# An attention and feed-forward layer on one core: weight pieces, first rows and last tiles placed elsewhere, the projection spread over four units, its reciprocal root on VectorE

## The chip, the cores and the metric
One core of one Trainium2 chip. The metric is the time of one execution in device microseconds (us); of the kernel before three runs were taken.

## The reference
```
x = h                                              # [8, 1024, 512] f32
qvk = layernorm(x) @ Wqvk                          # 16 heads of 32; order q, v, k
w   = softmax(causal(q k^T) / sqrt(512))
x   = x + layernorm((w v) @ Wo)
t   = layernorm(x) @ W1 + b1                       # 2048 wide
t   = t + (cos(th) wr + sin(th) wi) * wi * sin(th + 0.1 t) * 0.1
x   = x + layernorm(relu(t) @ W2 + b2)             # layernorm: eps 1e-5, no gain or bias
```
th, wr and wi are the quantum phases and weights.

## The kernel before
All products are done in float16 pairs: a number is split in a high and a low half, and three of the four cross products are added (PASSES), so one float32 product is three matmuls. There are three phases, one block each (`qkv_phase`, `attention_phase`, `ffn_phase`), and every engine's order of work is written out by hand; all DMAs are issued by SP, in order, and an engine or SP that waits holds up all that stands behind it.

**QKV** works in 16 chunks of 512 rows. A chunk has 12 products m of 12 matmuls each: 8 for q and k (`stage`, a ring of four, stored to `qk_parts` in DRAM), 4 for v. ScalarE writes the high half, VectorE the low half. Beside them the next chunk's rows are normed, split (`upper`, `lower`) and turned by DMA (`turn`). The chunks from 6 on (PEELED = 5 batches of two chunks, outside the loop) also prepare the weights of the other phases. Nine pieces (Wo, four of W1, four of W2; 1 MB each) pass through three slots: first each is read for its largest magnitude (VectorE, `largest`, and for Wo `centre`), at MAX_CHUNK = 6 and m in MAX_M; then, after `scales` in chunk 9, each is loaded once more and split in halves (`piece_high`, `piece_low`), from chunk 10 at m in SPLIT_M, and stored to DRAM in `weights.parts`. `first_units` loads q, k, v and rows of the first two attention units, all at the head of chunk 9. The last chunk also computes the row maxima of the first unit.

**Attention** works batch by batch; a batch has four units of four heads, a unit 20 slots (STEPS: query columns c of 256, key tiles j). In a slot TensorE makes scores (L1095), ScalarE the exponentials (L1158) and the high half (L1168), GpSimd the low half (L1257, SBUF to SBUF), and TensorE, six slots later, the weighted sum with v (L1122). For the next unit, score pieces are made in `pw` (two banks) and reduced by VectorE (L229): three in each of the first four slots of a unit, one to three in the others up to slot 15. `normalise` and `turned` put the result in `oT`. The output projection of a batch comes as eight tiles of 128 rows, each 12 matmuls in one bank `pwo` (L1080), then on VectorE mean and variance (`wo_stats`), on GpSimd `wo_small` (add eps, power -0.5), on VectorE `wo_out`, and a store to `x1`. The slots are WO_AT = 10, 15, ..., 45, counted from the head of the batch's last unit, so tiles fall into that unit and the first two of the next batch. `Stage` holds the order of the first, the middle, the last batch and of the drain after it; the middle batches 1 to 6 are one loop of six turns. In the drain all tiles follow one another in `pwo`.

**The feed-forward phase** has 16 chunks of 512 rows and 16 column groups f each: `hidden` (L1592), the activation over ScalarE and VectorE, and two groups later `output` (L1602). It starts with its own loads in SP's order: rows of chunk 0, quarters of w1 and w2, turns, the rest of the weights, b2, rows of chunk 1. VectorE scales b2 before its first group. At the end `post_read`, `post_stats` and `post_residual` run over all four tiles of the last chunk, with one store of 1 MB.

Of the kernel before, what the change touches and what calls it, by code (L numbers as in the profile page):

```python
# [29 lines left out]
P = 128  # L30
# [45 lines left out]
MAX_M, SPLIT_M = (1, 5, 9), (3, 9)  # L76
MAX_CHUNK, SCALE_CHUNK, SPLIT_CHUNK = 6, 9, 10
VEC_CHUNK = 6
# [63 lines left out]
assert all(TURN_AT[t // TQ] < at < NS + TURN_AT[t // TQ] for t, at in enumerate(WO_AT))  # L142
TAIL = WO_AT_LAST[-1] + WO_STORE + 1 - NS
# [6 lines left out]
MS = 2.0 ** 14  # L150

# [92 lines left out]
def qkv_phase(nc, x, w_qvk, w_o, w1, w2, vectors, weights, units, qk_parts, v_parts):  # L244
# [6 lines left out]
    LOAD_CHUNK = 9  # L251
    SLOTS = 3
    PEELED = 5
# [16 lines left out]
    with ctx:  # L270
# [72 lines left out]
        def job_at(n, m):  # L343

            for first, chunk, at in ((0, MAX_CHUNK, MAX_M), (PIECES_W, SPLIT_CHUNK, SPLIT_M)):
                if n >= chunk and m in at:
                    piece = len(at) * (n - chunk) + at.index(m)
                    if piece < PIECES_W:
                        return first + piece
            return None  # L350
# [6 lines left out]
        with nc.Block() as block:  # L357
            @block.sync
            def _(sp):
# [87 lines left out]
                def first_units():  # L447
                    for s in stored:
                        sp.wait_ge(s, 16 * (QK // STAGE) * CPB + START)
                    for u in range(2):  # L450
                        for c in range(CPB):
                            load_qk(sp, units, qk_parts, 0, u, c, True)
                            load_qk(sp, units, qk_parts, 0, u, c, False)
                    sp.wait_ge(v_stored, 16 * CPB + START)
                    for u in range(2):
                        load_v(sp, units, v_parts, 0, u)
                    for t in range(2):
                        load_x(sp, units, x.rearrange("b (t p) d -> b t p d", p=P), 0, t)
# [19 lines left out]
                for i in range(BATCH - PEELED, BATCH):  # L478
                    for e in range(2):
# [3 lines left out]
                        if 2 * i + e == LOAD_CHUNK:  # L483
                            first_units()
# [310 lines left out]
            def _(pe):  # L795
# [66 lines left out]
                with pe.Fori(1, BATCH - PEELED) as i:  # L862
                    for e in range(2):
                        chunk(i, e, False)
# [5 lines left out]
class Stage:  # L870
# [16 lines left out]
    def tiles(self, u, k, lag):  # L887

        s = u * NS + k - lag
        for m, (this, before) in enumerate(zip(*self.wo_at)):  # L890
            if s == this + (UNITS - 1) * NS and self.this:
                yield 0, m
            if s == before - NS and self.before:
                yield -1, m

# [43 lines left out]
def attention_phase(nc, x, weights, units, qk_parts, v_parts, x1):  # L939
    PR, HR, YR = 10, 10, 4  # L940


    LIFT = 8 * math.log(2)
    CONST = 2

    ctx = ExitStack()
    with ctx:
# [18 lines left out]
        oT = sb("oT", [P, 2, GROUPS, SEQ], F16)  # L966
# [3 lines left out]
        small = sb("small", [P, YR, 2])  # L970
        half = sb("half", [P, 1])
        y = sb("y", [P, YR, D])
# [12 lines left out]
        stats_done, mv_done, small_done = sem("stats_done"), sem("mv_done"), sem("small_done")  # L985
        wo_done, y_done = sem("wo_done"), sem("y_done")
        y_stored = [sem(f"y_stored{b}") for b in range(YR)]

        x_v = x.rearrange("b (t p) d -> b t p d", p=P)

        with nc.Block() as block:
# [11 lines left out]

            def run_all(engine, run):

                run(0, FIRST)
                with engine.Fori(1, BATCH - 1) as i:
                    run(i, MIDDLE)
                run(BATCH - 1, LAST)
                run(BATCH, DRAIN)  # L1010

            @block.sync
            def _(sp):
                x1_v = x1.rearrange("b (t p) d -> b t p d", p=P)

                def run(i, stage):
                    for u, k in stage.slots:
# [15 lines left out]
                        for b, t in stage.tiles(u, k, WO_STORE):  # L1033
# [4 lines left out]
                            elif stage is not DRAIN:  # L1038
                                load_x(sp, units, x_v, i + b + 1, t + 2 - QT)
                        if k == MAX_AT:  # L1040
# [637 lines left out]
```

## Time and profile before
| | |
|---|---|
| runs | 3446.77 us median of 3 (3444.99 to 3449.8) |
| profiled execution | 3445.31 us, span 3443.5 us |
| TensorE busy | 3148.3 us (91%) |
| VectorE, ScalarE, GpSimd busy | 2237.1 (65%), 2070.4 (60%), 1327.9 us (39%) |
| mean granted TensorE clock | 0.973 |

The busy shares are means over three phases with different limits. In the rows below PE is TensorE, PEld its weight loads, DVE VectorE, ACT ScalarE, POOL GpSimd, SPq the DMA queue's issues; L1095 is line 1095; "idle <- X" says what an engine stood waiting for. Tile names begin with q_, a_, f_ for the three phases, u_ and w_ for what they share.

### The profile page before, as it was taken

The numbers are of one execution on the slowest core, as the hardware profiler recorded it, in microseconds if no ns is written. First come the engines' busy times: TensorE is split into PE (matmuls) and PEld (weight loads), VectorE is DVE, ScalarE is ACT, GpSimd is POOL, SyncE is SP. The second block draws the span as 40 slices with busy tenths as digits, with TensorE's granted clock in tenths as the row PEclk, the third lists the DMA queues.
The fourth block names the chain that finished last, engine by engine and source line by source line (L and its number), as shares of the span: only waits on it lengthen the run. The fifth ranks groups of instructions, "written<-read, shape, count | busy, mean of one in ns | idle before, by whom it ended". The sixth has DMA issues, their size and how long they took to land. (4 is left out here: it accounts for less than half of the span.)

```text
span 3443.5 us, 76542 instructions
## 1 busy us (share of the span) xinstructions
PE 3148.3 (91%) x29476; PEld 1797.2 (52%) x29476; DVE 2237.1 (65%) x4207; ACT 2070.4 (60%) x2451; POOL 1327.9 (39%) x718
## 2 busy tenths in 40 slices
PE   7999898999898989989899858999999999999998
PEld 3444344766666666767676623444444444444443
DVE  5455555777676777767677624666666666666665
ACT  3222332988888887979797924555555555555554
POOL 2000000988888897979798930000000000000000
PEclk9999999999999999999999978999999999999999
DMA  6578783122222222222222132111111111111110
GB/s 181 171 218 248 232 260 90 52 70 82 58 84 64 81 69 78 63 84 58 86 66 79 44 101 90 37 38 39 37 37 37 37 37 37 37 37 37 37 37 25
DMA packets 328304, 279.95 MB, mean 81 GB/s; under 512 B 151056, under 2 KB 270032, under 8 KB 325968
## 3 DMA queue, kind: packets, MB, share of 16 engines
q1 hardware_dynamic: 328016, 275.82, 27.8%
q8 instruction: 217, 3.56, 0.4%
q14 instruction: 71, 0.58, 0.1%
HBM read 148.87 MB, written 92.80 MB: 70 GB/s over the span
## 5 line engine op out<-in xcount | busy, mean ns | idle before, releaser
L1257 POOL TENSOR_TENSOR a_prob_lo<-a_prob,a_prob_hi 128x2048 f16<-128x2048 f32 (+2 forms) x448 | 1191.9, 2689 | 185.8 <-ACT a_prob_hi L1168 184.2
L229 DVE TENSOR_REDUCE u_mx<-a_pw 128x4 f32<-128x512 f32 (+1 forms) x1178 | 730.6, 657 | 166.4 <-PE a_pw L215 126.6
L1158 ACT ACTIVATE a_prob<-a_pst,a_lift,w_exp_scale 128x1024 f32<-128x1024 f32 (+1 forms) x640 | 709.6, 1124 | 207.5 <-PE a_pst L1095 101.4
L1592 PE MATMUL f_ph<-f_xT,f_w 128*128 128x512 f16 x3072 | 707.5, 380 | 26.9 <-DMA f_xT<-f_xh 26.9
L1602 PE MATMUL f_py<-f_w,f_act 128*128 128x512 f16 x3072 | 707.6, 380 | 25.0 <-DVE f_work L1445 12.3
L1168 ACT ACTIVATE a_prob_hi<-a_prob 128x2048 f16<-128x2048 f32 (+2 forms) x448 | 583.3, 1302 | 0.0
L1559 ACT ACTIVATE f_hidden_work<-f_ph,w_turn,w_fold 128x512 f32<-128x512 f32 x256 | 199.3, 779 | 582.8 <-PE f_ph L1592 582.3
L1403 POOL TENSOR_TENSOR f_ve<-f_mv,f_eps 128x4 f32<-128x4 f32 x32 | 9.0, 283 | 1329.9 <-DVE f_mv L1427 1329.9
L1122 PE MATMUL a_acc<-u_vt,a_prob_hi 128*128 128x33 f16 x9216 | 466.0, 178 | 49.8 <-POOL a_prob_lo L1257 28.7
L1592 PEld LDWEIGHTS f_ph<-f_xT,f_w 128*128 128x128 f16 x3072 | 301.3, 98 | 392.2 <-issue 31.8
L1602 PEld LDWEIGHTS f_py<-f_w,f_act 128*128 128x128 f16 x3072 | 299.0, 98 | 395.4 <-issue 17.7
L1122 PEld LDWEIGHTS a_acc<-u_vt,a_prob_hi 128*128 128x128 f16 x9216 | 432.0, 96 | 132.2 <-DVE a_o L1199 28.7
L1095 PE MATMUL a_pst<-u_qp,u_kp 98*128 98x256 f16 (+1 forms) x2560 | 460.8, 265 | 33.1 <-issue 17.7
L210 PE MATMUL a_pw<-u_kp,u_qp 96*128 96x128 f16 (+1 forms) x1488 | 444.7, 334 | 50.5 <-DVE u_mx L229 31.7
L1122 PE MATMUL a_acc<-u_vt,a_prob_lo 128*128 128x33 f16 x4608 | 439.7, 178 | 0.0
L1122 PEld LDWEIGHTS a_acc<-u_vt,a_prob_lo 128*128 128x128 f16 x4608 | 366.8, 96 | 0.0
L803 PE MATMUL q_pm<-q_xT,q_w 128*128 128x512 f16 x1536 | 343.2, 385 | 25.5 <-DMA q_xT<-q_xh 21.3
L1472 DVE TENSOR_SCALAR f_hidden_work<-f_hidden_work 128x512 f32<-128x512 f32 x256 | 108.3, 423 | 380.9 <-ACT f_hidden_work L1559 378.9
L1095 PEld LDWEIGHTS a_pst<-u_qp,u_kp 98*128 98x128 f16 x2560 | 205.0, 98 | 119.4 <-issue 20.9
L803 PEld LDWEIGHTS q_pm<-q_xT,q_w 128*128 128x128 f16 x1536 | 151.3, 99 | 213.6 <-issue 32.4
L750 ACT ACTIVATE q_stage<-q_pm 128x512 f16<-128x512 f32 x128 | 76.3, 597 | 283.3 <-PE q_pm L803 244.4
L1080 PE MATMUL a_pwo<-w_wo,a_oT 128*128 128x512 f16 x768 | 196.7, 395 | 15.1 <-DVE a_y L1224 15.1
(161 smaller groups left out, 3345.7 us busy)
## 6 DMA issues: line engine op xcount, KB each, us to landing
qk_parts<-q_stage SPq DMA_DIRECT2D x128, 256.0 KB, 2.9
u_qp<-qk_parts SPq DMA_DIRECT2D x192, 128.0 KB, 2.7
u_kp<-qk_parts SPq DMA_DIRECT2D x192, 128.0 KB, 2.8
v_parts<-q_vstage SPq DMA_DIRECT2D x16, 1056.0 KB, 5.2
u_vt<-v_parts SPq DMA_DIRECT2D x32, 528.0 KB, 4.8
q_x<-in_L_attn_h_dram SPq DMA_DIRECT2D x16, 1024.0 KB, 8.6
q_raw<-in_L_ffn_W_dram SPq DMA_DIRECT2D x16, 1024.0 KB, 7.7
u_xr<-in_L_attn_h_dram SPq DMA_DIRECT2D x64, 256.0 KB, 3.1
```

Source lines behind the costliest of these rows:

```text
L210: last = pe.matmul(out[:, s * n:(s + 1) * n], units.qp[b][0:KQ, h, i * P:(i + 1) * P], units.kp[b][0:KQ, h, half_ * CH:half_ * CH + n], st ...
L229: dve.tensor_reduce(out, src[:, 0:n * len(heads)].rearrange("p (h n) -> p h n", n=n), AX_X, ALU.max).then_inc(units.released, 1)
L803: return pe.matmul(pm[:, m % BANKS, :], lhs, rhs, **flags)
L1080: last = pe.matmul(pwo[:, :], oT[:, a, g, t * P:(t + 1) * P], wo[:, w, g, :], start=(g == 0 and (w, a) == PASSES[0]), stop=(g == GROUPS - ...
L1095: last = pe.matmul(pst[:, slot, h, off:QC], kp[b][:, h, j * P:(j + 1) * P], qp[b][:, h, c * QC + off:(c + 1) * QC], start=(h == heads[0]), ...
L1122: last = pe.matmul(acc[:, (t * HPG + h) * VF:(t * HPG + h + 1) * VF], part[:, k % HR, h, t * P:(t + 1) * P], vt[:, b, j, col:col + VF], st ...
L1158: act.activation(prob[:, k % PR, :, off:QC], pst[:, k % 2, :, off:QC], ACT.Exp, scale=exp_scale, bias=lift[:, :]).then_inc(exp_done, 1)
L1168: act.activation(prob_hi[:, first % HR:first % HR + steps, :, off:QC], prob[:, first % PR:first % PR + steps, :, off:QC], ACT.Copy).then_i ...
L1257: pool.tensor_tensor(prob_lo[:, first % HR:first % HR + steps, :, off:QC], prob[:, first % PR:first % PR + steps, :, off:QC], prob_hi[:, f ...
L1559: act.activation(arg[:, s, :], ph[:, f % HB, :], ACT.Identity, bias=turn0[:, f:f + 1], scale=fold[:, 0:1]).then_inc(arg_done, 1)
L1592: last = pe.matmul(ph[:, f % HB, :], w1s[:, a, k, f * P:(f + 1) * P], xT[:, e, b, k, :], start=(j == 0), stop=(j == len(terms) - 1))
L1602: last = pe.matmul(py[:, t, :], act_r[:, f % AR, b, t * P:(t + 1) * P], w2s[:, a, f, :], start=(f == 0 and j == 0), stop=(f == NF - 1 and ...
```

## The change
Constants and placement:
```diff
-MAX_M, SPLIT_M = (1, 5, 9), (3, 9)
-MAX_CHUNK, SCALE_CHUNK, SPLIT_CHUNK = 6, 9, 10
-VEC_CHUNK = 6
+MAX_AT_OUTPUT = [(2 + n // 2, (3, 9)[n % 2]) for n in range(PIECES_W)]
+SPLIT_AT_OUTPUT = [(8, 3), (8, 9), (9, 3), (9, 9)] + [(n, 3) for n in range(10, 15)]
+JOBS = {at: job for job, at in enumerate(MAX_AT_OUTPUT + SPLIT_AT_OUTPUT)}
+SCALE_CHUNK = 7
+VEC_CHUNK = 2
-WO_AT = list(range(10, 10 + 5 * QT, 5))
-WO_AT_LAST = WO_AT
-WO_STATS, WO_SMALL, WO_OUT, WO_STORE = 2, 2, 4, 5
+WO_AT = list(range(10, 10 + 8 * QT, 8))
+WO_AT_LAST = [10, 15, 20, 21, 25, 26, 28, 29]
+OWN_BANK = {3: 0, 4: 1, 5: 2, 6: 3}
+WO_STATS, WO_OUT, WO_STORE = 2, 6, 7
+LAST_OUT, LAST_STORE = 3, 4
+ROOT_STEPS = 8
+ROOT_AT = {(2, 1): (0,), (3, 0): (1,), (3, 1): (2,), (4, 0): (3,), (4, 1): (4,), (5, 0): (5,), (5, 1): (6,), (6, 0): (7,)}
...
-    LOAD_CHUNK = 9
+    LOAD_CHUNK = 10
-    PEELED = 5
+    PEELED = 7
```
Chunks are outside the loop from 2 on. `first_units` comes in three parts, at the heads of chunks 10, 11 and 12: q and k of unit 0 (12 DMAs), of unit 1 (12), then v and rows (4).

Attention: the loop has three turns of two batches, with `oT` a group longer so that a batch's first group doesn't overwrite what the previous batch's last tiles still read. GpSimd's `wo_small` goes; eight operations on VectorE take its place, one at a time before or after the score maxima of slots +2 to +6 after the tile's, and all at once in the drain:
```diff
             def run_all(engine, run):
-                run(0, FIRST)
-                with engine.Fori(1, BATCH - 1) as i:
-                    run(i, MIDDLE)
-                run(BATCH - 1, LAST)
-                run(BATCH, DRAIN)
+                run(0, FIRST, 0)
+                with engine.Fori(0, BATCH // 2 - 1) as pair:
+                    run(2 * pair + 1, MIDDLE, 1)
+                    run(2 * pair + 2, MIDDLE, 0)
+                run(BATCH - 1, LAST, 1)
+                run(BATCH, DRAIN, 0)
...
+                def wo_root(i, t, step):
+                    v, y0, h0, y1, h1, slope, bow, y = (root[:, t % YR, c:c + 1] for c in range(ROOT_STEPS))
+                    if step == 0:
+                        dve.wait_ge(mv_done, n + 1)
+                        dve.tensor_tensor(v, mv[:, t % YR, 1:2], eps, ALU.add).then_inc(root_step, 1)
+                        return
+                    dve.wait_ge(root_step, ROOT_STEPS * n + step)
+                    if step == 1:
+                        dve.tensor_scalar(y0.bitcast(I32), v.bitcast(I32), -0.5, float(ROOT_BITS), ALU.mult, ALU.add
+                                          ).then_inc(root_step, 1)
+                    elif step == 2:
+                        dve.scalar_tensor_tensor(h0, y0, v, y0, ALU.mult, ALU.mult).then_inc(root_step, 1)
+                    elif step == 3:
+                        dve.scalar_tensor_tensor(y1, h0, -ROOT_NEAR, y0, ALU.add, ALU.mult).then_inc(root_step, 1)
+                    elif step == 4:
+                        dve.scalar_tensor_tensor(h1, y1, v, y1, ALU.mult, ALU.mult).then_inc(root_step, 1)
...
```
(steps 5 to 7: a tensor_scalar, a tensor_tensor, a scalar_tensor_tensor.) In the drain tiles 3 to 6 write to the four banks of `pst`, free by then, instead of `pwo`.

First rows of the feed-forward phase: a new object `Feed` holds its buffers that live from attention on (rows, halves, turned rows `xT` of chunk 0, a quarter of w1 and of w2, b2, statistics). In the last batch's last unit, slot 2, SP loads rows of chunk 0, those quarters and b2; the statistics come at slot 14, GpSimd's root at 15, the scaling at 18 (into two free slots of `prob`), the halves and the four turns at slot 2 of the drain. In the feed-forward phase only w1 and w2 from the second quarter on are loaded, and the wait for the x1 stores stands there, behind the first of these loads and ahead of the rows of chunk 1.
```diff
                         if in_last(stage, u, k, FEED_LOAD):
...
+                            load_rows(sp, feed, x1[2:BATCH + 2].rearrange("b (c t p) d -> (b c) p t d", p=P, t=TPC), 0, 0)
+                            for n in range(KT):
+                                sp.dma_start(feed.w1[:, :, n, :], weights.parts[n][:, :, 0:FF // 4]
+                                             ).then_inc(feed.w1_loaded, 16)
+                        if in_last(stage, u, k, FEED_HALVES):
+                            for t in range(TPC):
+                                turn_rows(sp, feed, feed.xT, 0, 0, t)
```
Last chunk: both last output groups are made tile by tile, and each tile is finished and stored by itself.
```diff
+                def last_outputs(n):
+                    for f in range(NF - LAG, NF):
+                        pe.wait_ge(act_lo, NF * n + f + 1 + START)
+                    for t in range(TPC):
+                        for f in range(NF - LAG, NF):
+                            for j, (a, b) in enumerate(PASSES):
+                                last = pe.matmul(py[:, t, :], act_r[:, f % AR, b, t * P:(t + 1) * P], w2_of(a, f),
+                                                 start=False, stop=(f == NF - 1 and j == len(PASSES) - 1))
+                        last.then_inc(w2_done, 1)
+                def last_rows(n, e):
+                    number = 2 * n + 1
+                    for t in range(TPC):
+                        dve.wait_ge(w2_done, TPC * n + t + 1 + START)
+                        dve.tensor_tensor(work[:, t, :], py[:, t, :], b2s[:, :], ALU.add).then_inc(y_read, 1)
+                        dve.wait_ge(y_read, TPC * n + t + 1 + START)
+                        dve.bn_stats(stats[:, 0, t, :], work[:, t, :]).then_inc(stats_done, 1)
...
+                        if t > 0:
+                            last_row(n, e, t - 1)
+                    last_row(n, e, TPC - 1)
```

## Rows read from the trace of the kernel before
**Rows 1.** Windows: stretch, length, busy us (count) per engine, clock, DMA.
```profile
592.20:2003.02 1410.82, 1260.40 (x20731) 948.80 (x20729) 1002.27 (x2008) 1203.36 (x1087) 1224.03 (x561) 0.97 0.24 69
```
**Rows 2.** Windows of units: fourth with loop-back, fourth without, first, second, third.
```profile
1063.42:1111.76 48.34, 39.07 (x626) 28.95 (x624) 31.75 (x64) 37.75 (x35) 43.48 (x20) 0.93 0.26 78
1788.26:1830.90 42.64, 39.18 (x670) 29.73 (x666) 31.74 (x64) 37.88 (x35) 37.95 (x19) 1.00 0.24 69
1111.76:1161.79 50.03, 46.24 (x697) 33.26 (x695) 34.68 (x73) 38.19 (x35) 34.61 (x21) 0.96 0.24 69
1161.79:1206.80 45.01, 40.91 (x678) 30.67 (x679) 34.15 (x69) 37.70 (x36) 39.31 (x19) 1.00 0.28 84
1206.80:1244.64 37.84, 34.86 (x612) 27.31 (x610) 28.48 (x57) 37.05 (x35) 37.11 (x15) 0.96 0.20 60
```
**Rows 3.** Waits of TensorE: who, for whom, us in total, times, longest.
```profile
PE a_pst L1095 <- issue: 17.7, 5, 3.7
```
**Rows 4.** Windows of QKV: chunk 5, chunks 6 to 14, chunk 9, chunks 10 to 14.
```profile
183.50:214.58 31.08, 31.08 (x145) 14.10 (x144) 15.22 (x29) 9.25 (x16) 1.41 (x3) 1.00 0.60 170
214.58:531.78 317.20, 288.66 (x1297) 127.93 (x1296) 186.88 (x327) 101.06 (x156) 12.69 (x27) 0.96 0.85 249
321.65:366.34 44.69, 32.70 (x144) 14.26 (x145) 18.92 (x48) 8.81 (x17) 1.41 (x3) 0.90 0.98 253
366.34:531.78 165.44, 160.13 (x720) 71.11 (x721) 96.47 (x158) 62.53 (x88) 7.05 (x15) 0.97 0.79 243
```
**Rows 5.** Waits of ScalarE.
```profile
ACT q_stage L750 <- DMA qk_parts<-q_stage: 38.5, 8, 20.8
```
**Rows 6.** Timeline of VectorE in chunk 6: start, length, what [idle before].
```profile
224.40 2.29 DVE L669 TENSOR_REDUCE q_row_mean<-q_raw 128x4 f32<-128x2048 f32 x1 [3.12 <-DMA q_raw<-in_L_attn_Wo_dram]
```
**Rows 7.** Timeline of VectorE between attention and feed-forward part.
```profile
2012.54 0.20 DVE L1197 RECIPROCAL a_rden<-a_acc 128x8 f32<-128x8 f32 x1
...
2041.74 0.70 DVE L1214 BATCH_NORM_STATS2 a_stats<-a_pwo 128x6 f32<-128x512 f32 x1 [4.21 <-PE a_pwo L1080]
...
2043.65 0.75 DVE L1224 SCALAR_TENSOR_TENSOR a_y<-a_pwo,a_small,u_xr 128x512 f32<-128x512 f32 x1 [0.93 <-POOL a_small L1268]
...
2084.34 0.49 DVE L1514 TENSOR_SCALAR f_b<-f_b,w_fold 128x512 f32<-128x512 f32 x1 [21.46 <-DMA f_b<-in_L_ffn_b_dram]
```
**Rows 8.** Chain of waits at the start of the feed-forward part.
```profile
2068.60 10.84 PE f_ph L1592 x36
2079.43 10.33 issue
```
**Rows 9.** Windows: slots 0-4, 5-9 of a first unit, then of a third.
```profile
1111.76:1127.03 15.27, 14.99 (x216) 10.63 (x215) 10.77 (x21) 9.28 (x10) 5.13 (x5) 0.88 0.03 9
1127.03:1137.97 10.94, 9.92 (x136) 6.82 (x134) 8.50 (x20) 8.63 (x9) 9.51 (x6) 1.00 0.45 126
1206.80:1216.47 9.67, 9.43 (x171) 7.28 (x168) 8.55 (x16) 8.96 (x10) 9.18 (x5) 1.00 0.17 49
1216.47:1224.97 8.50, 7.54 (x122) 5.57 (x122) 7.46 (x16) 8.42 (x10) 8.32 (x4) 1.00 0.36 106
```
**Rows 10.** Timeline of VectorE: small operations, each waiting for the one before.
```profile
235.11 0.17 DVE L616 TENSOR_SCALAR q_tmp<-q_tmp 128x16 f32<-128x16 f32 x1
235.32 0.17 DVE L617 TENSOR_SCALAR q_tmp<-q_tmp 128x16 f32<-128x16 f32 x1
```
**Rows 11.** Waits of VectorE.
```profile
DVE a_y L1224 <- POOL a_small L1268: 41.8, 36, 5.3
```
**Rows 12.** Timeline of VectorE and SP at the end.
```profile
3427.68 2.56 DVE L1445 TENSOR_TENSOR f_work<-f_py,f_b 128x512 f32<-128x512 f32 x4 [0.98 <-PE f_py L1602]
...
3438.89 0.38 SPq L1356 DMA_DIRECT2D out_dram<-f_work  x1
```
**Rows 13.** Durations min/median/max of the power in the feed-forward part.
```profile
L1405 POOL TENSOR_TENSOR f_rstd<-f_ve,f_half x32: 1009/1457/1462, 2056.6 to 3433.6; 128x4 f32<-128x4 f32 x32
```
**Rows 14.** Durations min/median/max of GpSimd's low halves.
```profile
L1257 POOL TENSOR_TENSOR a_prob_lo<-a_prob,a_prob_hi x448: 1147/2136/4107, 595.2 to 2009.3; 128x2048 f16<-128x2048 f32 x63, 128x1024 f16<-128x1024 f32 x44, 128x512 f16<-128x512 f32 x43
```

More of the change, by code:

```diff
@@ L343, in job_at @@
         def job_at(n, m):
[L345 to L350, printed above, removed]
+            return JOBS.get((n, m))
         def split_piece(piece, part):
@@ L894, in tiles, with last_batch @@
                 yield -1, m
+    def last_batch(self, b):
+        return (b == 0 and self.this and not self.after) or not self.this
     def shared_work(self):
@@ L969, in attention_phase @@
         mv = sb("mv", [P, YR, 2])
-        small = sb("small", [P, YR, 2])
-        half = sb("half", [P, 1])
-        y = sb("y", [P, YR, D])
+        root = sb("root", [P, YR, ROOT_STEPS])
+        y = feed.xin[:, 1]
         pw = ps("pw", [P, 2, CH])
@@ L1177, in run @@
                             high(i, *e)
+                        if in_last(stage, u, k, FEED_HALVES):
+                            act.wait_ge(feed.normed, 1)
+                            for t in range(TPC):
+                                act.activation(feed.xh[:, t, 0, :], rows[:, t, :], ACT.Identity, scale=XS
+                                               ).then_inc(feed.x_hi, 1)
                 act.wait_ge(const, CONST)
@@ L1225, in wo_out, with roots @@
                                              ALU.add).then_inc(y_done, 1)
-                def shared(i, at, before, what, unit, m, stage):
+                def roots(i, stage, u, k, late):
+                    for (lag, end), steps in ROOT_AT.items():
+                        for b, t in stage.tiles(u, k, lag):
+                            if end == late and not stage.last_batch(b):
+                                for step in steps:
+                                    wo_root(i + b, t, step)
@@ L1228, in shared, with run @@
+                def shared(i, at, before, what, unit, m, stage, parity):
                     bank = (work_before(0, stage) + at) % 2
                     if what == "turn":
-                        turned(i, unit, m, at, before, bank)
+                        turned(i, unit, m, at, before, bank, parity)
                     else:
                         maxima(i, at, before, what, unit, m, bank)
-                def run(i, stage):
+                def run(i, stage, parity):
                     before = work_before(i, stage)
@@ L1237, in run @@
                         for b, t in stage.tiles(u, k, WO_STATS):
-                            wo_stats(i + b, t)
+                            wo_stats(i + b, t, stage)
+                            if stage.last_batch(b):
+                                for step in range(ROOT_STEPS):
+                                    wo_root(i + b, t, step)
+                        roots(i, stage, u, k, 0)
                         for at, what, unit, m in stage.at(u, k):
-                            shared(i, at, before, what, unit, m, stage)
+                            shared(i, at, before, what, unit, m, stage, parity)
                         e = stage.earlier(u, k, LAG)
@@ L1568, in chunk @@
                             upper(i, n + 1, 1 - e, HALVES_AT[f])
-                act.wait_ge(normed, 1)
-                for t in range(TPC):
-                    act.activation(xh[:, t, 0, :], work[:, t, :], ACT.Identity, scale=XS).then_inc(x_hi, 1)
                 chunk(0, 0, True, False)
```

350 lines of the change are left out of this document (218 added, 132 removed).

## The prediction
> **What bounds the kernel now.** I read the windows by stage first, then the waits of TensorE, then windows cut to the kernel's own units. TensorE sets the pace throughout, but each stage leaks in its own way.
>
> Attention takes 1411 us [rows 1]: TensorE is busy for 1260, GpSimd 1224, ScalarE 1203, so three engines are near their limit together. Cut into units [rows 2], a unit with no output projection (third unit of a batch) takes 37.84 us, and there ScalarE (37.05) and GpSimd (37.11) are full. The unit with four projected tiles takes 50.03, those with two 45.01 and 42.64: there TensorE and VectorE carry the surplus. The last unit of a batch takes 48.34 where the loop jumps back behind it and 42.64 where it doesn't; TensorE's stall is "issue", five times [rows 3].
>
> QKV chunks should take 31.08 us, 144 matmuls at 0.216. The nine from 6 to 14 take 317.20 instead of 279.72, 37.5 too much: 13.6 in chunk 9 alone, 10.0 in 10 to 14, so 13.8 in 6 to 8 [rows 4]. In chunk 9 ScalarE stood 20.8 us for a store that sits in SP's queue behind 28 loads of the first units [rows 5]; in chunk 6 VectorE waits 3.12 us for the first weight piece and then reduces and centres it [rows 6], so rows are split and turned late.
>
> Between attention and the feed-forward part TensorE has almost nothing to do: the eight tiles' last y ends at 2044.40, the first feed-forward matmul starts at 2068.60, and after 36 matmuls it stops again for 10.33 us, because VectorE waits 21.46 us for b2 [rows 7, 8].
>
> **The change, part by part.** The sum is made against the profiled execution: 3445.3 us, of which 3443.5 is span; the median of the runs shown is 1.5 above it.
>
> *Pieces and loads in QKV.* Nine maxima go from three per chunk (6 to 8) to two per chunk (2 to 6), nine splits from two per chunk (10 to 14) to two in chunks 8 and 9 and one in 10 to 14, the scales from chunk 9 to an empty chunk 7, and the 28 loads become 12, 12 and 4 at chunks 10, 11, 12. The first piece is now wanted at m = 3 instead of 1, 5 us later, so the 3.12 us wait goes; the angles still come right before the centring. Before, nine maxima with that pile cost 13.8; with two per chunk I leave 4. Splits cost 10.0 for nine, 1.1 each; singles have more room: 6. Scales: 1. Twelve loads hold SP by proportion 20.8 x 12/28 = 8.9 us, and the ring of four stages covers four products, 10.4 us: 1 each, 3.5 with the large ones. That leaves 14.5 of 37.5: **-23**. Ends: -34 (as chunk 5) and -5 (every chunk like the average of 10 to 14 and the pile whole).
>
> *The batch loop* runs three times over two batches, so it jumps back twice, not five times. One jump costs 48.34 - 42.64 = 5.7 us [rows 2], and the slots behind it run at a granted clock of 0.88 [rows 9]; 6 each, **-18**. Ends: 0 (a body of twice the length stalls twice as long) and -20.
> The Trainium skill (Runtime: NRT & Kernel Launch, "Instruction fetch mechanics") says that a taken branch to code outside the fetch window stalls, and straight code streams. By that the price hangs on the number of jumps: -18 stands and the 0 end falls.
>
> *Projection over four units.* Tiles move from slots 10, 15 | 0, 5, 10, 15 | 0, 5 of four units to 10, 18 | 6, 14 | 2, 10, 18 | 6. Matmuls stay the same. Prices by slot: the first five slots of the four-tile unit take 15.27 against 9.67 without a tile, the next five 10.94 against 8.50 [rows 9]: 5.6 (some of it the slow clock; 4.5 without) for a tile at slot 0, 2.4 at slot 5. The early slots are dear since three score pieces each fill TensorE and VectorE there. Prices by unit: two tiles 4.8 to 7.2 over 37.84. Before, a batch takes 42.64 + 50.03 + 45.01 + 37.84 = 175.5. After, with 2, 2, 3 and 1 tiles at 2.4 each and slot 2 at 3.5: 151.4 + 20.3 = 171.7; with the two-tile unit's 42.64 as the measure, 42.64 + 42.64 + 45.1 + 40.2 = 170.6. Take -4.5 per batch.
> *Reciprocal root on VectorE.* Per tile eight [128 x 1] operations of 0.17 us, 0.21 from start to start [rows 10], 1.7 us, 13.4 per batch. VectorE's sum over four units is 129 of 175 [rows 2], so most lie beside other work; where they stand before a score maximum they hold a bank back. Lower bound 0, upper 13.4; I take 2.5, nearer to 0, since one step at a time is set between maxima. Removed are GpSimd's two operations and VectorE's wait for them, 41.8 us in 36 times [rows 11]; I count two thirds of it to the seven full batches, 4 each, a quarter of which TensorE pays today: -1 per batch. The y of a tile at slot 10 is now stored at slot 17, in SP's queue right ahead of the maxima that the next unit's scores need; its two issues cover under 1 us and two slots lie between. Together -3 per batch, seven batches: **-21**. Ends: -50 (roots free, TensorE without stalls) and +50 (roots in full, 13.4 - 5.5 = 8 per batch).
>
> *The last tiles and the first rows.* The accumulator of the last unit is read at 2012.54 [rows 7]. Then tiles 4 to 7 follow in banks of their own. TensorE is through with them in some 11 us; VectorE needs, per tile, stats 0.98, roots 1.7, y 0.75: 3.4, four times 13.6, after the first tile's 2.6 and the last turn's 0.9: 2029.6. The store is no longer waited for; 2.5 for the block's end and start: first feed-forward matmul at 2032 instead of 2068.6, -36.6. Rows are loaded, normed, split and turned in attention's last unit, where VectorE has time; a quarter of w1 and w2 and b2 too, so the 10.33 stall goes. **-47**. Ends: -52 and -35 (a fetch or transfer late at the start).
>
> *The end.* Both last products now wait for the later activation; then tiles are finished one by one. Before, VectorE's chain runs from 3427.68 to the store at 3438.89, 11.2 us [rows 12]. After: the first tile needs six matmuls behind that activation instead of three, so it is read 0.65 later, 3428.3. GpSimd's 1.4 of the 11.2 hides behind the next tile, 28 waits at some 0.05 add 1.4, and operations cut in four some 1.2: 12.4, the last store at 3440.7, of a quarter of the bytes, where the old one took the 4.6 to the span's end. **0** (-1.5 to +1.5).
>
> Sum: -23 - 18 - 21 - 47 = -109; 3445.3 - 109 = **3336**.
>
> **Rivals.**
> *A. GpSimd blocks the roots (slower).* Six of the eight root operations read two SBUF tensors while GpSimd subtracts in SBUF. Today attention has no such VectorE operation, so no row shows what one costs. What speaks for it: the feed-forward's pow takes 1009 ns alone and 1457 where VectorE runs two-input operations beside it [rows 13]: the two do get in each other's way. Against: the VectorE side isn't stretched there. If a root has to wait for the end of GpSimd's current operation, of 1147 to 4107 ns [rows 14], the mean rest is about 1.45 us at the present load; 48 such per batch make 70 us on a VectorE with 46 free: at least +24 per batch, seven times 168, on top of what is left of the rest (3336 + 21): **3525**. It decides slower from 1.22 us per root operation on: the other parts give 88, 12.6 per batch, and with the 46 free that is 58.6 over 48 operations.
> The Trainium skill (SBUF — State Buffer, "SBUF: two separate sides") states this as a rule: a VectorE operation with two SBUF inputs and a GpSimd operation that reads SBUF exclude each other for a whole instruction. By it 3525 would be the forecast; the unstretched VectorE side is why I don't follow it.
> *B. Spreading brings nothing:* roots at half their full price, 6.7 per batch, against -5.5: about +1, and loads crowd chunks 10 to 12 (-15 for QKV). 3445.3 - 15 - 18 + 7 - 47 = **3372**. For it: the early slots of even the tile-free unit are full on both engines [rows 9]. Against: the later slots are not.
> *C. All slack is used:* units near 42, QKV like chunk 5: 3445.3 - 34 - 20 - 40 - 50 = **3301**.
> *D. The change doesn't shorten the loop's stalls:* 3336 + 18 = **3354**.
>
> **How the numbers follow.** Forecast 0.5, A 0.12, B 0.14, C 0.12, D 0.12. The range 3290 to 3385 holds forecast, B, C and D with little cut off. The bound of no change is 0.2%, 7 us. Faster 0.88, same 0.01, slower 0.11 (A with little of its price left still lands below).
>
> **What would show it.** Chunks 6 to 9 near 31 us and no wait of ScalarE above 5 us for a store; two "issue" stalls in attention; unit times within 40 to 45 rather than 38 to 50; each root at 0.17 us with no idle time ascribed to GpSimd; first feed-forward matmul 2032 less what went before it, and 36 matmuls followed by outputs at once; the last store a few us before the end, as now. Wrong would be: root operations of over 0.5 us, VectorE full in attention, or TensorE waiting on maxima for over 15 us per batch.

## The result: slower by 6.1%, where the forecast said faster by 3.2%

| | before | after |
|---|---|---|
| median of the runs shown | 3447.7 us (3445.0 to 3449.8, 4 runs) | 3657.0 us (3654.4 to 3661.2, 4 runs) |
| span of the profiled execution | 3443.5 us | 3654.8 us |
| mean granted clock | 0.973 | 0.933 |

The ratio is 1.061, 95% interval [1.059, 1.063]; the forecast was 3336. It was rival A that came, and dearer than priced (3525).

First the page of the changed kernel: busy time by engine, and the span in 40 slices.

```profile
PE 3228.8 (88%) x29476; PEld 1843.6 (50%) x29476; DVE 2570.5 (70%) x4725; ACT 2078.3 (57%) x2451; POOL 1288.5 (35%) x595
...
PE   7999998878777788788778777999999999999998
...
DVE  5655456787787877877787885566666666666665
...
PEclk9999999989888898888889887999999999999999
```

The same matmuls take TensorE longer (the clock is lower in the middle slices), and VectorE is busy for 2570.5 us; the page of before had 2237.1. Nearly all of the surplus lies in slices 7 to 24, in the attention phase. Windows of the changed kernel: the whole phase (to be held against [rows 1]), then the first, second, third and fourth unit of a batch, and the fourth of the next, without a jump (against [rows 2]). Columns: stretch and length, then busy time of PE, PEld, DVE, ACT, POOL, the clock, the DMA share, GB/s.

```profile
578.00:2264.60 1686.60, 1350.67 (x20725) 995.86 (x20724) 1331.61 (x2486) 1213.45 (x1087) 1190.85 (x448) 0.87 0.21 60
955.70:1007.93 52.23, 43.82 (x672) 32.47 (x669) 43.78 (x89) 38.24 (x35) 33.45 (x14) 0.87 0.22 64
1007.93:1075.19 67.26, 48.14 (x664) 34.23 (x661) 53.58 (x87) 38.14 (x36) 41.15 (x16) 0.80 0.19 57
1075.19:1125.26 50.07, 41.32 (x682) 31.15 (x680) 40.83 (x81) 38.01 (x35) 33.37 (x14) 0.90 0.23 68
1125.26:1181.31 56.05, 42.17 (x625) 30.62 (x623) 40.46 (x71) 37.75 (x36) 42.04 (x16) 0.85 0.20 55
1346.50:1393.27 46.77, 40.18 (x627) 29.29 (x624) 35.86 (x71) 37.88 (x35) 41.26 (x16) 0.93 0.19 53
```

By stage: QKV ends 14.2 us earlier (592.2 to 578.0); attention takes 1686.6 instead of 1410.8, +275.8; from there (the last exp) to the second feed-forward chunk 111.8 instead of 159.2, -47.4; the rest 1278.4 instead of 1281.2, -2.8. Together that is the whole difference of the spans, 211.3. So one stage lost 276 and the others gained 64.

What fills VectorE is seen in its groups, by line and shape: busy us and mean ns of one, behind the bar. These are the eight root operations in order of cost, and TensorE's longest waits.

```profile
L1363 DVE SCALAR_TENSOR_TENSOR a_root<-a_root 128x1 f32<-128x1 f32 x64 | 82.1, 1283 | 0.3
L1368 DVE SCALAR_TENSOR_TENSOR a_root<-a_root 128x1 f32<-128x1 f32 x64 | 63.5, 992 | 0.5
L1373 DVE TENSOR_TENSOR a_root<-a_root 128x1 f32<-128x1 f32 x64 | 61.8, 965 | 0.4
L1375 DVE SCALAR_TENSOR_TENSOR a_root<-a_root 128x1 f32<-128x1 f32 x64 | 60.0, 938 | 2.2
L1356 DVE TENSOR_TENSOR a_root<-a_mv,w_wo_eps 128x1 f32<-128x1 f32 x64 | 39.7, 620 | 0.5
L1366 DVE SCALAR_TENSOR_TENSOR a_root<-a_root 128x1 f32<-128x1 f32 x64 | 28.1, 440 | 2.2
L1370 DVE TENSOR_SCALAR a_root<-a_root 128x1 f32<-128x1 f32 x64 | 9.8, 154 | 2.2
L1360 DVE TENSOR_SCALAR a_root<-a_root 128x1 int32<-128x1 int32 x64 | 9.8, 154 | 2.2
```
```profile
PE a_pw L296 <- DVE u_mx L315: 149.6, 101, 5.1
PE a_acc L1247 <- DVE a_o L1329: 92.9, 55, 9.3
PE a_pw L1188 <- DVE u_mx L315: 41.8, 44, 2.0
```

One element per partition, and a mean of up to 1283 ns: that is not work. The two operations with one SBUF input (L1360, L1370) take 154 ns in every one of 64 cases; of the six with two SBUF inputs 140 of 384 take over 300 ns, 293.0 us together, the longest 4.06. TensorE's wait for a bank of scores went from 31.7 to 149.6, its wait for a_o from 18.6 to 92.9.

The timelines show whom they wait for. VectorE in the last unit of the last batch, then GpSimd, then TensorE (start, length, what, idle before).

```profile
2251.94 0.16 DVE L1356 TENSOR_TENSOR a_root<-a_mv,w_wo_eps 128x1 f32<-128x1 f32 x1
2252.13 0.15 DVE L1360 TENSOR_SCALAR a_root<-a_root 128x1 int32<-128x1 int32 x1
2252.32 3.72 DVE L1363 SCALAR_TENSOR_TENSOR a_root<-a_root 128x1 f32<-128x1 f32 x1
2256.08 3.98 DVE L1366 SCALAR_TENSOR_TENSOR a_root<-a_root 128x1 f32<-128x1 f32 x1
2260.09 0.22 DVE L1368 SCALAR_TENSOR_TENSOR a_root<-a_root 128x1 f32<-128x1 f32 x1
...
2261.04 0.42 DVE L1329 TENSOR_TENSOR a_o<-a_acc,a_rden 128x256 f32<-128x256 f32 x1
```
```profile
2251.94 8.11 POOL L1444 TENSOR_TENSOR a_prob_lo<-a_prob,a_prob_hi 128x2048 f16<-128x2048 f32 x2 [2.61 <-ACT a_prob_hi L1293]
```
```profile
2261.61 0.21 PE L1247 MATMUL a_acc<-u_vt,a_prob_hi 128*128 128x33 f16 x2 [9.31 <-DVE a_o L1329]
```

GpSimd's two subtractions run from 2251.94 to some 2256.0 and on to 2260.05. The root's first operation, with two inputs, began at the same moment as the first subtraction and took its 0.16 us; the second, with one input, passes beside it. The third has two; it ends at 2256.04, the fourth at 2260.06. Behind them stand the reading of the accumulator and so TensorE, for 9.31 us. This holds throughout: all 140 long operations end within 21 ns of the end of one of GpSimd's subtractions. The other 244 show the same from the other side: 243 began while no subtraction ran (to within 30 ns), 36 of them after the last one, and the only one that lies inside a subtraction is the one above, begun within 1 ns of it.

### The profile page after: what moved, and what is told of

The parts are those of the page before. It is cut to its first block and busy times, and to the rows that moved or that the text cites. A ratio compares the mean times of both kernels' runs of the same rounds, so it can differ in the third digit from the quotient of the medians.

```text
span 3654.8 us, 76702 instructions
## 1 busy us (share of the span) xinstructions
PE 3228.8 (88%) x29476; PEld 1843.6 (50%) x29476; DVE 2570.5 (70%) x4725; ACT 2078.3 (57%) x2451; POOL 1288.5 (35%) x595
## 5 line engine op out<-in xcount | busy, mean ns | idle before, releaser
L296 PE MATMUL a_pw<-u_kp,u_qp 96*128 96x128 f16 (+1 forms) x1488 | 488.5, 363 | 153.9 <-DVE u_mx L315 149.6
L1247 PE MATMUL a_acc<-u_vt,a_prob_hi 128*128 128x33 f16 x9216 | 478.7, 181 | 112.6 <-DVE a_o L1329 92.9
L1247 PEld LDWEIGHTS a_acc<-u_vt,a_prob_hi 128*128 128x128 f16 x9216 | 450.5, 99 | 207.1 <-DVE a_o L1329 83.0
L1788 PE MATMUL f_py<-f_w,f_act 128*128 128x512 f16 x2280 | 523.1, 379 | 0.0
L1220 PE MATMUL a_pst<-u_qp,u_kp 98*128 98x256 f16 (+1 forms) x2560 | 495.6, 282 | 25.7 <-ACT a_prob L1283 11.3
L888 PE MATMUL q_pm<-q_xT,q_w 128*128 128x512 f16 x1536 | 342.5, 385 | 20.7 <-DMA q_xT<-q_xh 16.4
L1788 PEld LDWEIGHTS f_py<-f_w,f_act 128*128 128x128 f16 x2280 | 223.1, 98 | 269.0
L1220 PEld LDWEIGHTS a_pst<-u_qp,u_kp 98*128 98x128 f16 x2560 | 216.6, 103 | 127.4 <-issue 35.2
L1767 PE MATMUL f_ph<-s_xT,f_w 128*128 128x512 f16 x1152 | 264.3, 379 | 0.0
L1767 PE MATMUL f_ph<-f_xT,f_w 128*128 128x512 f16 x1152 | 264.3, 379 | 0.0
L296 PEld LDWEIGHTS a_pw<-u_kp,u_qp 96*128 96x128 f16 x1488 | 141.0, 104 | 215.0 <-DVE u_mx L315 173.2
```

The costliest lines, as they stand in the source:

```text
L296: last = pe.matmul(out[:, s * n:(s + 1) * n], units.qp[b][0:KQ, h, i * P:(i + 1) * P], units.kp[b][0:KQ, h, half_ * CH:half_ * CH + n], st ...
L888: return pe.matmul(pm[:, m % BANKS, :], lhs, rhs, **flags)
L1220: last = pe.matmul(pst[:, slot, h, off:QC], kp[b][:, h, j * P:(j + 1) * P], qp[b][:, h, c * QC + off:(c + 1) * QC], start=(h == heads[0]), ...
L1247: last = pe.matmul(acc[:, (t * HPG + h) * VF:(t * HPG + h + 1) * VF], part[:, k % HR, h, t * P:(t + 1) * P], vt[:, b, j, col:col + VF], st ...
L1767: last = pe.matmul(ph[:, f % HB, :], w1_of(a, k, f), xT[e][:, b, k, :], start=(j == 0), stop=(j == len(terms) - 1))
L1788: last = pe.matmul(py[:, t, :], act_r[:, f % AR, b, t * P:(t + 1) * P], w2_of(a, f), start=(f == 0 and j == 0), stop=(f == NF - 1 and j == ...
```

## The experiments

All twelve kernels copy the normed rows into xT instead of turning them, as their expectations say; two of them are the bases. Each edit below is against the base named. "From the start to the last unit" is from attention's first exp to that of the last batch's last unit.

**The bases.** In both kernels the two transfers into xT:

```
-    sp.dma_start(xT[:, e, :, :, t * P:(t + 1) * P], xh[...], transpose=True)
+    sp.dma_start(xT[:, e].rearrange("p b k c -> p (b k c)")[:, t * 2 * D:(t + 1) * 2 * D], xh[...])
```

> The kernel before, with the turn of the rows by DMA (SP's 256 KB transfers into xT, in the QKV and the feed-forward phase) replaced by a plain copy of the same 256 KB, so what is computed from those rows is not the reference's. It is the base against which the others of this kind are read. All theories: within 1% of 3447.7, rather below it, and the attention phase unchanged at 1370 from its start to the last unit of the last batch.

> The changed kernel with the same plain copy in place of the turn (what is computed from those rows is not the reference's), nothing else. Both theories: its distance to the kernel before with plain copies is again 209 +- 15, and the root operations with two SBUF inputs again stretch to about 4 us each while the two with one SBUF input stay at 0.15. If the distance falls below 150, the turning transfers take part in the loss and neither theory is whole.

Measured (each ratio is to the kernel before, run on the same chip): copy_before 3430.7 us (0.995 [0.993, 0.997]), 1371.0 from the start to the last unit; copy_after 3652.1 (1.059 [1.057, 1.060]), 1635.3. The distance is 221.3; 139 root operations of over 300 ns take 294.8 us. The turning transfers have no part in the loss.

**One SBUF input instead of two.** Against copy_after, six operations like this one:

```
-    dve.scalar_tensor_tensor(h1, y1, v, y1, ALU.mult, ALU.mult)
+    dve.tensor_scalar(h1, y1, v, y1, ALU.mult, ALU.mult)
```

> The changed kernel (plain copies) with the six root operations that read two or more SBUF tensors written as tensor_scalar: one tensor comes in as the stream, the others as per-partition scalars. Same eight steps, same places, same semaphores. Theory PORT (a VectorE operation with two SBUF streams waits until GpSimd's running operation has ended): all eight root operations then take 0.15 to 0.2 us, the 293 us of long ones go, and the kernel falls to 3310 to 3350. Theory PLACE (the loss is from the spread itself: outputs six units late hold the PSUM banks and stages, or eight small operations per tile break VectorE's stream): stays above 3600. A middle value says that the per-partition scalars count as streams in part.

Measured: 3364.8 us (0.975 [0.974, 0.977]), 1352.7 from the start to the last unit. All the groups of root operations:

```profile
L1368 DVE TENSOR_SCALAR a_root<-a_root 128x1 f32<-128x1 f32 x64 | 17.1, 267 | 0.5
L1363 DVE TENSOR_SCALAR a_root<-a_root 128x1 f32<-128x1 f32 x64 | 17.0, 265 | 0.3
L1375 DVE TENSOR_SCALAR a_root<-a_root 128x1 f32<-128x1 f32 x64 | 13.7, 214 | 2.3
L1366 DVE TENSOR_SCALAR a_root<-a_root 128x1 f32<-128x1 f32 x64 | 13.7, 214 | 2.2
L1373 DVE TENSOR_SCALAR a_root<-a_root 128x1 f32<-128x1 f32 x64 | 13.2, 207 | 0.4
L1356 DVE TENSOR_SCALAR a_root<-a_mv,w_wo_eps 128x1 f32<-128x1 f32 x64 | 13.2, 206 | 0.5
L1360 DVE TENSOR_SCALAR a_root<-a_root 128x1 int32<-128x1 int32 x64 | 9.8, 154 | 2.2
L1370 DVE TENSOR_SCALAR a_root<-a_root 128x1 f32<-128x1 f32 x64 | 9.8, 154 | 2.2
```

The same data, places and semaphores, 287 us less; the longest of the 512 takes 275 ns, although 280 of the 384 rewritten ones lie wholly inside a subtraction. TensorE's wait for maxima falls to 26.8. PORT holds, PLACE falls; the time is 15 above what I gave PORT. The operations that read values as per-partition scalars are a little longer by themselves (0.21 to 0.27 instead of 0.15 to 0.21) but never blocked. The Trainium skill (DVE: scalar operands, raw-bit mode, write accounting and state across instructions, "Pointer scalars") says that such a scalar does not take up the second tensor stream; this run agrees, and such an operation wasn't held up by GpSimd's subtractions either. Nor is it the kind of operation that blocks: in the changed kernel itself the 128 tensor_tensor operations (L1338) that make the low halves of a_oT from one PSUM and one SBUF tensor take 424 to 426 ns, and 83 of them lie wholly inside one of the same subtractions.

**The root back on GpSimd.** Against copy_after: wo_root and its places out, GpSimd's add and pow of before in, at two units of the slot list behind the projection.

> The changed kernel (plain copies) with its reciprocal root put back on GpSimd as add and pow, at two units behind the projection, and everything else of the spread (projection every eight units, output at +6, store at +7) left. PORT: no two-stream operation of VectorE is left in a unit, so 3310 to 3360, within 25 of the one-input version. PLACE: above 3600, since the spread is all there.

Measured: 3344.2 us (0.969 [0.968, 0.971]), 1336.1 from the start to the last unit. As PORT said. So with nothing blocked the eight operations on VectorE cost 20.6 us more than two on GpSimd (16.6 of it up to the last unit).

**The root alone, in the kernel before.** Against copy_before: wo_root in place of wo_small, with

```
+ROOT_AT = {(2, 1): (0, 1), (3, 0): (2, 3), (3, 1): (4, 5), (4, 0): (6, 7)}
```

> The kernel before (plain copies) with only the reciprocal root changed: its eight root operations on VectorE in the changed kernel's form (six with two SBUF streams), two steps at each of four places between the projection and the output four units later; projections still five units apart. Base 3430.7 (attention start to last unit 1371.0). PORT: the loss needs nothing of the spread, so it comes here too: GpSimd's subtractions run through the same units, 3580 to 3730, with root operations of up to 4 us that end with a subtraction. Rival SPREAD: the long operations hurt only because they sit in every unit of a batch and the output is six units late; here with five-unit spacing it is within 30 of base.

> The same as before_roots with each of the eight steps as a one-stream tensor_scalar. PORT: every step 0.15 to 0.28; 1.68 per tile as measured in one_input, so 6.7 per batch on VectorE, part of it hidden: 3435 to 3460 against the base of 3430.7. SPREAD: the same 0 to 30. If it came out below the base, taking two operations and their waits off GpSimd would be a gain by itself.

Measured: before_roots 3711.6 us (1.074 [1.070, 1.078]), 281 over copy_before; before_one_input 3479.4 (1.010 [1.008, 1.011]), 48.7 over it. In before_roots 127 root operations are long, 267.8 us, all ending within 20 ns of a subtraction's end. The first of the eight:

```profile
L1228 DVE TENSOR_TENSOR a_root<-a_mv,w_wo_eps 128x1 f32<-128x1 f32 x64 | 99.7, 1558 | 0.2
```

The root alone makes the loss, with no spread: PORT's range. The one-input form cost more than I had expected (3435 to 3460, at most 29 over the base): in pairs, in the units that already carry four and two tiles, the small operations are not hidden (first unit 54 instead of 50, batch 187 instead of 181.5). In the spread they cost 20.6.

**The dose.** Against one_input, step 2 alone as scalar_tensor_tensor again.

> The one-input version with a single root operation of the eight (step 2) put back to two SBUF streams: the dose. Base 3364.8. PORT: this operation waits for the end of the subtraction then running on GpSimd, which is busy for most of a unit, so 30 to 50 of its 64 runs are long (1 to 4 us each), 40 to 80 of VectorE time and, as VectorE's maxima feed TensorE, most of it in the span: 3395 to 3440. A sixth of the 287 that separate copy_after from one_input would be 48: 3413. Rival CHAIN (only long chains of such operations hurt, a single one is absorbed): 3365 to 3375.

Measured: 3445.5 us (1.000 [0.999, 1.001]), 80.7 over one_input, 5 above my range. Its group, and TensorE's wait for maxima:

```profile
L1363 DVE SCALAR_TENSOR_TENSOR a_root<-a_root 128x1 f32<-128x1 f32 x64 | 91.7, 1433 | 0.3
```
```profile
PE a_pw L296 <- DVE u_mx L315: 84.0, 108, 3.2
```

48 of 64 are long. The operation takes 74.7 us more than its one-input form, the span grows by 80.7: all of it, although VectorE is busy for only 1150 of attention's 1472 us. One is enough, and one of six costs more than a sixth (81 of 287), since 48 of its 64 were caught, where in copy_after 139 of 384 were. There GpSimd is busy for less of the phase (1191 of 1687 us in the changed kernel, 1185 of 1472 here), so an operation meets it idle more often; whether that is the whole reason wasn't tested.

**Shorter subtractions.** Against copy_after:

```
-    pool.tensor_tensor(prob_lo[..., :, off:QC], prob[...], prob_hi[...], ALU.subtract).then_inc(lo_done, 1)
+    pool.tensor_tensor(prob_lo[..., :half, off:QC], prob[...], prob_hi[...], ALU.subtract)
+    pool.tensor_tensor(prob_lo[..., half:, off:QC], prob[...], prob_hi[...], ALU.subtract).then_inc(lo_done, 1)
```

> The changed kernel (plain copies, two-input roots as they were) with each GpSimd subtraction issued as two of half the size, one behind the other. Base 3652.1. Theory OPERATION: VectorE waits for the end of the one GpSimd operation that is running, then goes between two: the longest root operation falls from 4.1 to about 2.1 us, the 293 of long ones to 130 to 200, the kernel to 3480 to 3570. Rival BACKLOG: VectorE waits until GpSimd has nothing left to run: the longest stays at 4 us or grows, and the kernel at 3640 or above.

Measured: 3565.9 us (1.035 [1.033, 1.037]), 86 below copy_after; 186 long operations, 234.3 us. All but one are at most 2.12 us long, and all end within 21 ns of the end of a subtraction. The one, and what GpSimd does meanwhile:

```profile
2138.91 10.33 DVE L1356 TENSOR_TENSOR a_root<-a_mv,w_wo_eps 128x1 f32<-128x1 f32 x1
```
```profile
2137.35 2.14 POOL L1445 TENSOR_TENSOR a_prob_lo<-a_prob,a_prob_hi 128x1024 f16<-128x1024 f32 x1
2139.45 2.12 POOL L1448 TENSOR_TENSOR a_prob_lo<-a_prob,a_prob_hi 128x1024 f16<-128x1024 f32 x1
2141.53 1.16 POOL L1445 TENSOR_TENSOR a_prob_lo<-a_prob,a_prob_hi 128x512 f16<-128x512 f32 x1
...
2147.10 2.12 POOL L1448 TENSOR_TENSOR a_prob_lo<-a_prob,a_prob_hi 128x1024 f16<-128x1024 f32 x1
```

OPERATION holds for 176 of 186, BACKLOG doesn't. But nine operations saw one subtraction end before theirs, and this one saw seven end and GpSimd take the next each time. What decides then who goes first is open; with subtractions of full size, no operation saw more than one end. The loss in the sum (234, forecast 130 to 200) was larger than I said: more operations are caught (186 instead of 139), each for less (1.26 us instead of 2.12 in the mean).

**The rest of the change.** The loop against copy_before, the QKV phase against copy_before, the spread and the last two jumps against root_on_pool:

```
-    with engine.Fori(1, BATCH - 1) as i: run(i, MIDDLE)
+    with engine.Fori(0, BATCH // 2 - 1) as pair: run(2 * pair + 1, MIDDLE); run(2 * pair + 2, MIDDLE)
```
```
-MAX_CHUNK, SCALE_CHUNK, SPLIT_CHUNK = 6, 9, 10
+MAX_AT_OUTPUT, SPLIT_AT_OUTPUT, SCALE_CHUNK, LOAD_CHUNK, PEELED = ..., ..., 7, 10, 7
```
```
-WO_AT = list(range(10, 10 + 8 * QT, 8))      WO_OUT, WO_STORE = 6, 7
+WO_AT = list(range(10, 10 + 5 * QT, 5))      WO_OUT, WO_STORE = 4, 5
```
```
-    with engine.Fori(0, BATCH // 2 - 1) as pair:
+    for pair in range(BATCH // 2 - 1):
```

> The kernel before (plain copies) with the loop over the six middle batches run as three turns of two batches. The prediction gave the loop three jumps back fewer at about 6 each, 18 in all: 3409 to 3416, with two instead of five issue stalls and the fourth unit 42.6 in every second batch. Rival: code loading stays in the way (twice the code per turn), no gain or a loss: 3425 to 3445.

> The kernel before (plain copies) with the changed kernel's QKV phase only: where weight pieces are reduced, scaled and split, which chunk loads the first units, seven chunks written out. Prediction's term: 23 less, so 3408. What the changed kernel's trace showed instead: attention starts 8 to 14 earlier: 3417 to 3425. Rival: nothing, since the start of the attention phase waits on its first loads: 3428 to 3434.

> The version with the root on GpSimd, with the spread undone: projections five units of the slot list apart, output at +4, store at +5 as before. Base 3344.2. It gives what the spread is worth once nothing blocks VectorE. The prediction's term was 4.5 per batch, some 31: 3365 to 3380. Rival: the spread is worth nothing by itself (the projections only change place in a full TensorE stream): within 8 of base.

> The version with the root on GpSimd and the loop over pairs of batches written out, so no jump back in the attention phase (three pairs; two jumps go). Base 3344.2. By the fourth units with and without the jump (46.3 to 47.1 against 41.5 to 43.2) each costs 4: 3334 to 3338. Rival: the longer code costs its own loading, no gain: 3342 to 3350.

Measured: before_pairs 3406.2 us (0.988 [0.987, 0.990]), -24.5; before_qkv 3411.7 (0.990 [0.988, 0.991]), -19.0; pool_root_five_apart 3352.6 (0.973 [0.971, 0.975]), so the spread brings 8.5; pool_root_unrolled 3326.3 (0.965 [0.963, 0.967]), another -17.9 for the last two jumps.

A jump costs 8 to 9 us in these runs (24.5 / 3, 17.9 / 2), not 6. The stalls are only a part. With the old QKV phase there are two at each jump, less than 4 us apart, not one; these are TensorE's rows in copy_before, then in before_qkv:

```profile
PE a_pst L1095 <- issue: 16.8, 5, 3.6
PE a_pw L210 <- issue: 13.7, 5, 3.0
```
```profile
PE a_pst L1093 <- issue: 20.9, 5, 4.4
```

That is 6.1 us per jump with the old QKV phase and 3.9 in root_on_pool (7.8 for two). In pool_root_unrolled the fourth units take 41.5 throughout, in root_on_pool 46 to 47 before a jump, but the batch behind a jump is longer in its first unit too (45.1 against 43.8). Of before_qkv's 19, only 7.4 lie in QKV; 12.0 lie in attention, of which it changes nothing: the units with a jump take 46.4 instead of 48.6. The rows above show where most of that comes from: the second stall is gone at all five jumps and the first is a little longer, 9.7 us less in all. Why another QKV phase takes a stall out of the attention loop is open. The last kernel is the fastest that was run: 104 below copy_before.

## Why the prediction was wrong

**The step that failed** is the roots' term, which left out that a root waits for GpSimd's subtraction: "Lower bound 0, upper 13.4; I take 2.5, nearer to 0", with duration 0.17 us from a one-input operation [rows 10] for six operations with two. The row's 0.17 us holds only for an operation that isn't blocked: in the changed kernel the six took 0.87 us each in the mean, and the roots cost 308 us (copy_after against root_on_pool). Without the block the term would have been off by its size alone: 2.5 for the roots less 1 for GpSimd's two operations is 10.5 for seven batches, and one_input against root_on_pool, which measures just that difference, gives 20.6. The row nearest to them was in no part of the attention phase, and the upper end should have come from the subtractions, which last up to 4107 ns [rows 14].

**Why rival A was put down.** I held against it that "the VectorE side isn't stretched" beside the pow [rows 13]. For the pow that reading was right. In the kernel before, VectorE and then GpSimd in the feed-forward phase:

```profile
2125.75 0.69 DVE L1458 TENSOR_TENSOR f_act<-f_hidden_work,f_act 128x512 f16<-128x512 f32 x1
```
```profile
2125.22 1.46 POOL L1405 TENSOR_TENSOR f_rstd<-f_ve,f_half 128x4 f32<-128x4 f32 x1
```

L1458 reads two SBUF tensors, begins 0.53 us into the pow and takes the 0.68 to 0.69 us that it takes everywhere; so it is beside 30 of the 32 pows, and beside 30 of 31 in the changed kernel. What failed was to carry this over from a pow on [128 x 4] to a subtraction on up to [128 x 2048], beside which the kernel before has no such operation: an absence of rows was taken for evidence. The Trainium skill (SBUF — State Buffer, "SBUF: two separate sides") gives the rule for just this pair of instructions, a lock that whoever starts first keeps for the whole instruction; all 140 ends within 21 ns agree. Two things go against its letter, and the measurement decides: L1458 isn't held up by a pow that started before it, and the 10.33 us operation had to wait on when a subtraction had ended. What sets the pow apart, its few elements or its operation, was not tested.

**Rival A's price** was wrong in both factors. It took each of 48 operations in a batch as waiting 1.45 us, 70 in all; measured is 37 per batch (293.0 over eight), since only 140 of 384 were caught, for 2.1 us each; the others began between two subtractions. And it let VectorE's 46 free us swallow the greater part; they swallowed nothing. The two errors went against each other, so that 3525 came as near as it did is in part luck. For the same reason its threshold failed, "slower from 1.22 us per root operation on": 0.87 made the kernel slower by 6.1%. one_of_six shows it by itself (+74.7 on VectorE, +80.7 in the span), and so does the unit table: VectorE is busy for 43.8 of 52.2 us while TensorE waits. Free time elsewhere in a unit doesn't help a score maximum that stands behind a blocked operation. "VectorE full in attention" was the wrong sign to look for; "root operations of over 0.5 us" and "TensorE waiting on maxima for over 15 us per batch" were the right ones (149.6 + 41.8 over eight batches is 24).

**QKV, -23, measured -14.2.** Chunks 6 to 14, the nine that the term was made for:

```profile
220.26:517.51 297.25, 283.97 (x1297) 127.31 (x1296) 163.23 (x293) 99.81 (x153) 12.64 (x27) 0.98 0.81 230
314.47:350.92 36.45, 31.24 (x144) 14.04 (x145) 22.93 (x42) 12.90 (x18) 1.97 (x5) 0.97 0.85 268
350.92:390.01 39.09, 33.35 (x145) 14.54 (x146) 17.24 (x30) 11.02 (x17) 2.13 (x5) 0.94 0.98 283
```

They fell from 317.20 [rows 4] to 297.25, -20.0; chunks 6 and 7 are at 31.08, chunk 9 is still at 36.45 and chunk 10, with the first twelve loads, at 39.09. ScalarE's waits for a store in chunk 2 (window 90:126) and in chunk 10 (window 350:392):

```profile
ACT q_stage L835 <- DMA qk_parts<-q_stage: 9.2, 1, 9.2
```
```profile
ACT q_stage L835 <- DMA qk_parts<-q_stage: 4.9, 1, 4.9
```

Behind the twelve loads of chunk 10 ScalarE waits 4.9 us for a store, so the four stages cover a part of the 8.9 worked out, not all of it. The longest wait, 9.2 us, has nothing to do with these loads: it comes at 111.26, in chunk 2. What the term left out is that the maxima now stand in chunks 2 to 6: chunk 6 starts at 220.26 instead of 214.58, 5.7 later, most of it in chunks 2 and 3, which take 34.4 and 32.8.

**The loop, -18.** Two "issue" stalls instead of five (6.6 us instead of 17.7 [rows 3]), as said, and the kernel before had five more that no row ahead of the prediction shows, 12.8 us for a_pw, of which the changed kernel has none. The loop was worth 24.5 alone, so more than the unit with a jump shows by itself. The first stall doesn't double with a body of twice the length (3.3 us against 3.5; 3.7 in before_pairs against 3.4 in copy_before), so the end of 0 falls. The Trainium skill (Runtime: NRT & Kernel Launch, "Instruction fetch mechanics") says that a taken branch to code outside the fetch window stalls; that the cost goes by the number of jumps agrees with it, at 8.2 us each for three fewer and 9.0 each for the last two. **The spread, -4.5 per batch or 31**, was 8.5 by pool_root_five_apart. The early slots' price of 5.6 was read from the unit behind the jump, where part of it was the jump's.

**The last tiles and the first rows, -47.** The chain of waits at the start of the feed-forward part:

```profile
2295.36 10.61 PE f_ph L1767 x36
2305.97 0.51 issue
2306.48 2.75 PE f_py L1788 x12
```

Against [rows 8]: 0.51 instead of 10.33, and the first matmul comes 30.8 us behind the last exp, where 29.0 was worked out and 65.6 stood before. That makes the -47.4 of the table by stages, but flatters it: the last exps were themselves late, behind the blocked roots (that unit took 53.8 us, before it was 40.3). From the start of the last unit to the second feed-forward chunk it is 199.5 before and 165.6 after, -33.9; from copy_before to one_input, where nothing is late, 196.0 and 159.6, -36.4. The term was 11 too large. The window between the last exp and the first feed-forward matmul of one_input:

```profile
1961.70:2003.70 42.00, 22.42 (x206) 11.12 (x206) 32.73 (x86) 3.61 (x6) 8.52 (x4) 0.78 0.25 87
```

VectorE is busy for 32.7 of its 42.0 us: it has more to do there than the 17.1 (13.6 + 2.6 + 0.9) that I counted. **The end, 0:** the last chunk takes 104.3 instead of 104.1.

So the other terms were right in sign, and the sum without the block can be read from one_input against copy_before: -66 where it said -109. By the spans of these two traces the gap is 44.3: QKV 15.9 (attention starts 7.1 earlier, not 23; with the turning transfers it was 14.2), attention 20.7 (18.3 instead of 39), the last tiles 10.6, and 2.9 given back by the rest. In attention, up to the last unit, the single runs give for the spread 9.7 instead of 31, for the roots less GpSimd's two operations 16.6 lost instead of 10.5, for the loop 24.4 instead of 18: together 17.5, near the 18.3, although the 12.0 that before_qkv gained there isn't in that sum, so the parts don't simply add. My sizes were too hopeful even where the mechanism was right.

## What to carry to other kernels

Before work is moved to VectorE beside a busy GpSimd, count the SBUF tensors that each operation reads: with two, even one element per partition waited here for the end of GpSimd's running subtraction, so price it by GpSimd's longest, not by its own length. Don't take a short GpSimd instruction beside which nothing waits as a sign that a long one is harmless too. Written as tensor_scalar with the other values as per-partition scalars, the same arithmetic wasn't blocked. Where an engine's queue feeds the engine that sets the pace, its free time in the sum covered nothing here of what blocked it in the middle.

## What the runs showed of the hardware

- A [128 x 1] operation of VectorE with two SBUF inputs took up to 4.06 us beside subtractions of up to 4.10, and once 10.33 us across seven shorter ones; with one SBUF input 153 to 155 ns at all times, with per-partition scalars at most 275 ns.
- A [128 x 512] operation with two SBUF inputs was not held up by a GpSimd pow on [128 x 4] that had begun 0.5 us earlier: 683 to 694 ns in 30 cases, as in all 256.
- GpSimd lost nothing: its 448 subtractions took 1204.6 us with the blocked roots, 1206.2 without.
- Halving GpSimd's instructions gave 86 us back without touching VectorE.
- TensorE's granted clock fell with its stalls: 0.87 over attention in the changed kernel, 0.98 in one_input with the same matmuls, busy for 1350.7 and 1252.7 us.
- The jump back of a loop cost 8 to 9 us per turn. TensorE's stalls at it were 6.1 us in copy_before, in two pieces, and 3.9 in root_on_pool, in one; the units behind it were longer too.
